# Handing out fewer filler steps at three places of an eight-core Mamba and mixture-of-experts layer

## What is computed

```python
xn = layernorm(x)                                    # x: (8, 2048, 1024)
zxbcdt = xn @ in_proj_w                              # 1024 -> 4384
z, xBC, dt = split(zxbcdt, [2048, 4352])
xBC = silu(conv_b + sum_k shift(xBC, k) * conv_w[3 - k])
x_part, B, C = split(xBC, [2048, 2176])
dt = softplus(dt + dt_bias); A = -exp(A_log)
state = state * exp(A * dt_t) + (x_t * dt_t) B_t     # over 2048 steps, 32 heads of 64, state 128
y_t = state C_t
g = (y + x_part * D) * silu(z)
attn = (g * rsqrt(mean(g**2) + eps) * norm_w) @ out_proj_w
logits = xn @ gate_w.T; w, sel = top_k(logits, 2); w = softmax(w)
ffn = sum over the two chosen experts of w * (xn @ expert_w[e].T)
out = x + attn + ffn
```

## Time and profile before

| | us |
|---|---|
| median of the runs (2000.69 to 2000.94) | 2000.82 |
| the profiled execution, its own time | 1997.9 |
| its span on the slowest core (1977.5 to 1996.3 over the cores) | 1996.3 |
| matrix engine busy (of the span) | 1139.1 (57%) |
| vector engine busy | 831.2 (42%) |
| scalar engine busy | 666.7 (33%) |
| of the matrix engine: expert groups L642, 4096 matmuls | 585.5 |

### The profile page before, as it was taken

The page is one execution under the profiler, slowest core; times in us unless marked ns, Lnnn a source line. Parts: engine busy times, 40 slices in busy tenths (PEclk is TensorE's granted clock), DMA queues, the critical chain, the costliest instruction groups (busy, mean ns, idle before and its releaser), DMA issues.

```text
span 1996.3 us, 26303 instructions; the slowest of 8 cores (1977.5 to 1996.3 us)
## 1 busy us (share of the span) xinstructions
PE 1139.1 (57%) x7995; PEld 784.8 (39%) x7995; DVE 831.2 (42%) x1772; ACT 666.7 (33%) x1356; POOL 0.2 (0%) x4
## 2 busy tenths in 40 slices
PE   1110265686667756676658665866586677665320
PEld 1110143454444544454436444644364445442100
DVE  3643423544344433543365226522643254424525
ACT  2343154124521352226313532254125422452110
POOL 0000000000000000000000000000000000000000
PEclk9999999888997889888989887998798888898655
DMA  6842000000000100000001000000100000000069
GB/s 165 276 178 84 27 17 24 22 27 25 27 22 22 48 25 19 27 22 30 19 22 54 27 22 22 30 27 24 40 27 28 21 27 24 25 14 22 5 204 306
DMA packets 64942, 103.78 MB, mean 52 GB/s; under 512 B 8870, under 2 KB 49958, under 8 KB 62246
## 3 DMA queue, kind: packets, MB, share of 16 engines
q1 hardware_dynamic: 60198, 89.51, 14.3%
q10 hardware_dynamic: 4608, 12.58, 1.6%
HBM read 85.28 MB, written 16.78 MB: 51 GB/s over the span
## 4 chain that ended last, share of the span: by engine, by line
PE 42%; ACT 14%; DVE 13%; issue 9%; DVEq 4%; SPq 3%; ACTq 3%; DMA 1%
PE P L642 15%; ACT DGS L764 7%; PE P L823 6%; PE P L1086 6%; PE P L739 5%; PE P L775 4%; DVEq L72 4%; ACT AC L787 2%; ACTq L72 2%; DVE SCR L1033 2%; DVE Y L1028 2%; SPq L1173 2%; DVE OACC L663 2%; PE P L1068 1%; DVE Y L1039 1%
## 5 line engine op out<-in xcount | busy, mean ns | idle before, releaser
L642 PE MATMUL P<-EWB,XN 128*128 128x256 bf16 x4096 | 585.5, 299 | 33.6 <-DVE EWB L613 29.8
L642 PEld LDWEIGHTS P<-EWB,XN 128*128 128x128 bf16 x4096 | 437.0, 108 | 154.1 <-issue 51.0
L663 DVE SCALAR_TENSOR_TENSOR OACC<-P,WFULL,OACC 128x256 bf16<-128x256 f32 x448 | 215.1, 482 | 610.7 <-PE P L642 590.8
L775 PE MATMUL P<-XB,DGS 128*128 128x256 bf16 x576 | 100.5, 304 | 196.4 <-ACT DGS L764 196.1
L764 ACT ACTIVATE DGS<-IBF,CW 128x128 bf16<-128x128 bf16 x576 | 184.8, 391 | 15.7 <-PE P L642 3.0
L823 PE MATMUL P<-WIN,XN 128*128 128x512 bf16 x512 | 127.3, 393 | 74.8 <-DVE SZ L860 40.5
L739 PE MATMUL P<-XN,WIN 128*128 128x256 bf16 x1152 | 140.3, 276 | 25.7 <-ACT XB L750 10.6
L775 PEld LDWEIGHTS P<-XB,DGS 128*128 128x128 bf16 x576 | 53.2, 105 | 236.6 <-issue 227.4
L739 PEld LDWEIGHTS P<-XN,WIN 128*128 128x128 bf16 x1152 | 111.2, 99 | 50.4 <-issue 35.5
L787 ACT ACTIVATE AC<-P,CB 128x256 bf16<-128x256 f32 x144 | 68.6, 476 | 178.9 <-PE P L775 155.4
L1075 ACT COPY SCR<-P 128x2048 bf16<-128x2048 bf16 x16 | 29.9, 1867 | 292.8 <-PE P L1068 292.8
(11 more groups left out here) (123 smaller groups left out, 965.9 us busy)
## 6 DMA issues: line engine op xcount, KB each, us to landing
ESTG<-we SPq DMA_DIRECT2D x256, 128.0 KB, 2.2
XR<-x SPq DMA_DIRECT2D x32, 512.0 KB, 7.0
WSTG<-wi SPq DMA_DIRECT2D x8, 1098.0 KB, 7.7
WSTG<-wi SPq DMA_DIRECT2D x8, 1078.0 KB, 8.5
WOSTG<-wo SPq DMA_DIRECT2D x16, 512.0 KB, 4.7
out<-OST ACTq DMA_DIRECT2D x16, 512.0 KB, 7.9
attd<-ATTS ACTq DMA_DIRECT2D x16, 256.0 KB, 2.0
oaccd<-OACC SPq DMA_DIRECT2D x4, 1024.0 KB, 4.4
```

The costliest lines, as they stand in the source:

```text
L642: li = e.matmul(pp4[:, of4:of4 + 256], XN[:, k * L + t * 128:k * L + (t + 1) * 128], EWB[:, eb * 2048 + k * 256:eb * 2048 + (k + 1) * 256] ...
L663: return e.scalar_tensor_tensor(OACC[:, t * 256:(t + 1) * 256], pp4[:, of4:of4 + 256], WFULL[:, t * 8 + ee:t * 8 + ee + 1], OACC[:, t * 25 ...
L775: li = e.matmul(cvp[:, cvo:cvo + 256], DGS[:, j * 128:(j + 1) * 128], XB[:, ct * XBW + 4 - dd: ct * XBW + 260 - dd], start=(dd == 0), stop ...
```

## The change

Three numbers: behind each z group one step instead of two, behind the gtr transposes two instead of four, behind the output projection three instead of five. No instruction is added or removed; the steps that are not handed out there are handed out by later calls, or by the last one.

```diff
@@ -829,7 +829,7 @@
                                     mz = st("T", zmm,
                                             waits=[st_c01[0], m_szprev[0]])
-                                    drip(2)
+                                    drip(1)
                                     yield
@@ -1070,7 +1070,7 @@
                     mgt = st("T", gtr, waits=[mep, st_c23[0]])
-                    drip(4)
+                    drip(2)
                     yield
                     ev_gfm = st("S", lambda e: e.copy(SCR[:], P23B[:, 0:2048]),
                                 waits=[mgt])
@@ -1093,7 +1093,7 @@
                     mop = st("T", opmm, waits=[ev_gfm] +
                              (wom if c == 0 else []))
                     m_op[c] = mop
-                    drip(5)
+                    drip(3)
                     yield
```

## The result

The changed kernel takes 2043.78 us in the median, the kernel before 2000.82: a ratio of 1.0211 [1.0187, 1.0234], 42 us more. The forecast was 2025 with a range to 2042; the time lies 1.8 us above the range, and the interval of the ratio lies on both sides of 2%. The sign was right, the amount was not.

The account below looks back on a forecast made before the run. No engine is full, so chains of waits bound the kernel, and filler counts only where it lengthens one. Terms -8.0 + 0 + 3.0 + 8.1 + 4.3 + 16.8 gave +24: 2025 us, range 2003 to 2042.

Parts of the forecast that it names:

- The count of the steps: Of 1540 expert steps the pairs hand out 1504 after the change; 36 are left for the last call.
- the final block: Leftover expert work behind the last projection: 16 groups at full clock, first load of the next block 15.8 us later.
- The price of a group: Each expert group costs 0.87 us of the matrix engine at the full clock.
- Chunk 15: Its back, running alone, is filled with 26 steps up to its projection: +4.3 us, bounds 2 and 7.
- a z step as work is free: Behind z groups, filler does not set the wait; taking 64 steps out saves 0 to 2 us, taken as 0.
- the clock term in z: Less filler in the z stretches leaves more idle time and some slow clock: +3 us, between 0 and 15.
- The prediction's own sign of being wrong: Wrong if pairs shorten by over 3 us each, z intervals grow towards 5.1, or final groups take 1.7 us.
- The clock rival: z stretches go to the low clock and the final block stays there: 2051 us, chance 0.14.
- the body outside z: Fewer groups behind transposes and output projections, gtr and op sites: 8 us saved, bounds 4 and 14.
- the third block: After the final block, OACR waits for the last dump, which lands in 4.4 us; +1.0 us taken.
- The last pair: The last two chunks, unfilled before, get 49 steps at 0.165 us a step: +8.1 us.
- the Faster rival: Matrix engine order sets the pace everywhere, last chunks swallow the work; 118 steps save 34 us: 1984 us, chance 0.08.

Follow-up runs that it names:

- e2: Kernel before with only the gtr and op calls thinned, to 2 and 3 steps, z left at 2: 2000.21 us, 0.9986.
- e1: Kernel before with only the z call thinned, one step instead of two, gtr and op left at 4 and 5: 2013.92 us, 1.0051.
- e3: Changed kernel plus four matmuls of 256 columns, result never read, behind each z group: 2036.7 us, 1.0167 against the kernel before.
- e7: Kernel before with no step behind the z groups, gtr and op left at 4 and 5: 2058.52 us, 1.027.
- e8: Kernel before with two steps handed out ahead of the first front, all calls unchanged: 2014.37 us, 1.0056.
- e4: Changed kernel with three steps instead of two behind every second convolution tile: 2019.25 us, 1.0077 against the kernel before.
- e5: Kernel before with gtr and op at 2 and 3, three steps behind every second convolution tile: mean span of cores 0 to 3 1996.5 us, before 1988.9.
- e6: Like e5, but one step instead of two behind each projection wave, four instead of three behind every second convolution tile: 2027.62 us, 1.0102, wide interval.
- e9: Kernel before with one step instead of two behind each projection wave, three instead of two behind every second convolution tile: 1987.54 us, 0.9948.
- e10: Kernel before with gtr and op at 2 and 3, projection wave at 1, every second convolution tile at 3, z at 3: 1975.48 us, 0.9877.
- e11: Changed kernel plus four matmuls of 256 columns, result never read, behind gtr of even chunks: 2034.41 us, without an interval.

## Why the prediction missed

**Right.** The count of the steps: 36 left, 16 groups of them in the final block, as in the timeline above. The price of a group at the full clock. The final block, forecast at +15.8 to the first load: +14.7. Chunk 15, forecast +4.3: +4.1. That the block stays at the full clock. That L775 follows an odd projection with one group in between, 7.8 us behind its start (core 4):

```profile
893.18 7.07 PE L1086 MATMUL P<-WOUT,SCR 128*128 128x512 bf16 x32
900.09 1.04 PE L642 MATMUL P<-EWB,XN 128*128 128x256 bf16 x8
900.96 0.60 PE L775 MATMUL P<-XB,DGS 128*128 128x256 bf16 x4
```

Summed over the sites that the prediction named, transposes to projection gained 2.0 (even) and 3.8 us (odd) and odd projection to L775 3.4: 9.2 us against 8.0. And that a z step as work is free: 3.56 against 3.55.

**Failed: the clock term in z, +3.0, measured +12.4.** The mechanism stood in the prediction with both prices; the size was chosen wrongly, at two points. "The convolution stays mostly at the full clock with less matmul per us than z will have" took a mean over 74 us of a stretch with short gaps as a guide for a stretch whose gaps are 2.3 us long. By the busy times of the earlier trace rows the comparison was not safe even so: 50.18 of 74.20 us is 0.68, and z's 24.03 us less the 2.3 us of filler that eight steps hold is 0.62 of 35.00. And 3 us were some two newly slow groups a core, where there were 11.9; at the 1.5 us of the earlier trace rows that would even have been 18, but the mean price is 1.05. The rows held the warning: the earlier trace rows show a slow z group behind an idle 2.29, and taking a group out of the half boundary turns 1.61 into about that at every boundary where two had stood. The prediction's own sign of being wrong, z intervals that grow towards 5.1, came: behind 99 firsts of 256 they are 4.6. The clock rival put z at +15, and that half of it came about. Its other half, the final block at half clock, did not.

The Trainium skill (TensorE: Matmul & The Clock Gate, Part 1) has half rate as the default state, which activity releases; the prediction set this against its rows, and in direction the trace agrees, with 99 slow first groups instead of 22. What the prediction made of it, that the z stretches would go slow, went too far: 157 of 256 stayed fast.

**Failed: the body outside z, -8.0, measured +2.0.** The 9.2 us are there, and went to two places. The even projections took the low clock over from the filler: even projection to the next matmul grew by 3.7 us over seven pairs (4.1 in e2, which has these two edits alone, -1.7 in e1, which has neither). The prediction had written "two groups cost 1.1 us, one nothing" and put at nothing what the groups did for the projection behind them, though the earlier trace rows has both, 7.07 behind a filled and 8.60 behind an unfilled gap. The second place is the step from the last convolution tile to the first z group, 19.2 us before and 25.6 after over eight pairs, +6.4. Its timeline on core 4:

```profile
750.85 1.01 PE L775 MATMUL P<-XB,DGS 128*128 128x256 bf16 x4 [2.92 <-ACT DGS L764]
751.66 3.62 PE L642 MATMUL P<-EWB,XN 128*128 128x256 bf16 x16
```

Two groups now stand there, at half clock, in front of the first z group. Neither e1 (19.9) nor e2 (19.5), which have the edits apart, has that, while e3, with the order of the change, does (25.6), and e7 and e8 with no edit ahead of that place have 22.0 and 21.8; e4, e5, e6, e9 and e10 hand out a step or two more just behind the last tile and don't tell. So where the pattern of six stands when the pair gets there is the likely cause. -9.2 + 3.7 + 6.4 is +0.9, the remaining 1.1 is spread. With the 5 us of scatter that e3 shows, more than "the saving was lost" isn't shown: e1 and e2 have bodies 6.5 and 7.2 us shorter, and if these added up the change should have 14. That the phase is the cause of the difference is what e8 suggests (11 us for two steps), but no run has the change with 188 steps a pair in another phase, so its part in the change itself stays argued.

**Off in size: the third block, +1.0, measured +3.8.** Of it 2.7 is the wait of OACR for the last dump: XR to OACR is 1.9 to 2.1 in the kernels whose dump is issued earlier and 4.0 to 4.7 in after, e3, e7 and e11. The prediction let the loads of the first tile cover most of 4.4 us; XR takes its place in the queue 0.7 us behind the dump, and in the slowest case the dump lands in 6.0. **The last pair, +8.1, measured +4.7**; the kernels with 188 to 197 steps a pair lie at +4.1 to +8.9, so 0.165 us a step was fair and its spread wider than given.

Two slips in the working changed little: three even chunks at 1.1 us are 3.3, not 3.0, and the Faster rival's 118 steps hold 44 groups by the prediction's own count, not 39, which makes 38 us of its 34.

Of the 17 us missing, z has 9.4, the body 10.0, the third block 2.8; the last pair gives back 3.4, the final block 1.1 and the start 0.7. The range was too narrow because its upper end held one miss at a time: z at its bound and the body at none of its saving were each inside, together they were outside.

## What to carry over

Filler on the matrix engine has a price that depends on the place: here 0.20 to 0.40 us a step among back-to-back projection waves (e9, e10, e6), in the convolution 0.06 to 0.09 for a third step behind a tile (e9, e5, e10; in e4 the stage got shorter) and 0.26 for a fourth (e6), and below zero for the first two in the z stretch, where they hold the clock. So before a call is thinned, ask what each idle gap becomes and which real work stands behind it, and count where the steps run out: moved steps come back at the end at their full price. Of the versions here e10 is the fastest, with one step in the projection, three in the convolution and three behind z: 1975.5 us, 1.2% below the kernel before. It carries gtr and op at 2 and 3; the same kernel with 4 and 5 was not run.

## What the runs showed of the hardware

- A stretch whose gaps between z groups are 1.6 to 2.3 us long stood at a granted clock of 0.79, with z groups at half clock in a row; others of the same kernel stood at 0.89 to 0.95. With 156 matmuls in such a stretch instead of 108 the clock was 1.00, for the same busy time (e10).
- In these kernels the low clock behind a long idle time falls on whichever matmuls come first. After 10.54 us of idle and 16 transposes two expert groups take 3.27 us and the projection 7.07; after 11.34 us of idle and 16 transposes, with no group between, the projection takes 8.84.
- 128 expert matmuls without a gap ran in 14.13 us on each of the eight cores, 110 ns each for 256 columns, at the full clock, the blocks of the cores starting within 15 us.
- Two steps more at the start, out of 1540, cost 11 us (1.0056 [1.0024, 1.0088]): this interleave has a phase.
